# Fusing the base projection and the experts' first layer into one stage, with the experts' second layer as plain products and weight splits in a ring of halves

## The chip, the cores and the metric

The kernel runs on one core of a Trainium2 chip. The metric is the device time of one execution in microseconds (us). A core has a matrix engine (TensorE, PE in the profile, with its weight loads as PEld), a vector engine (VectorE, DVE), a scalar engine (ScalarE, ACT), a general one (GpSimd, POOL) and a queue engine (SyncE, SP). Each runs its own instructions in order, and they meet through semaphores. On-chip memory has 128 partitions; the matrix engine writes its sums into 8 banks of 512 fp32 values per partition.

## The reference, cut to what matters

```python
# x: (32, 64, 1024) fp32; cond: 32 indices in 0..15
a = einsum('bct,bcd->bdt', x, L0_cond_weights[cond])            # mixing, 64x64 per sample
h = silu(a @ w1.T + b1) * (a @ w2.T + b2)                        # "up": 1024 -> 2 x 1024
x = x + h @ w3.T + b3                                            # "down"
y = x @ W + (x @ lora_A[cond]) @ lora_B[cond]                    # "lin", rank 16 per sample
base = y @ W_org.T
coeffs = softmax((y.mean(1) @ Wq.T) @ lora_keys.T / sqrt(128))   # 8 experts per sample
hh = einsum('bsi,eir->bser', y, lora_down)                       # "expin": 1024 -> 8 x 64
x = x + base + einsum('be,bser,ero->bso', coeffs, hh, lora_up)   # "expup": 512 -> 1024
```

## The kernel before

The 2048 tokens go in two halves of 1024 (`HALVES`), each in two tiles of 512 (`TN`). Activations lie transposed: features on partitions, tokens along the row. A half runs through seven stages (`KINDS`, line 46): `up0`, `up1`, `down`, `lin`, `expin`, `base`, `expup`. Before `up0` comes the mixing (`mixing`, 128 small products of 128x128 fp32 per half).

Each stage is a 2 by 2 block product done with Strassen-Winograd: 7 products (`PRODUCTS`) instead of 8, of the four weight blocks W11, W12, W21, W22 and the four activation blocks, and of their sums. The sums S1 to S4 of activations (`s_sum`) and T1 to T4 of weights (`t_sums`) are made on DVE. Every operand is split into a high and a low fp32r part: ACT casts the high part (`act.copy` in `s_split` and `t_split`, lines 579 and 591), DVE subtracts it to get the low one (line 675). A product is then `groups * pairs * 3` matmuls of 128x128 weights on 512 columns (lines 450 to 452): 4 groups, 4 pairs and so 48 matmuls in a full stage, 24 in `expin` (2 groups) and in `expup` (2 pairs). A group fills one bank. ACT copies a product's banks out (`snap`) or DVE adds them to a block (`add`, line 754; with a bias, `addb`, line 766); in the up stages ACT applies silu (line 611) and DVE the gate (line 782).

The order of the work is written out by hand: each engine has a loop over the products `n`, and in it stands what that engine does beside product `n`: the splits of product `n + 1`, the rest of product `n - 1`, the sums. Splits have two buffers, used in turn by product. The weights have five buffers of 1 MB (the fifth, `WE`, holds T2). In `lin`, the rank-16 terms are two further kinds of matmul in plain fp32: `lora_in` (line 493, 8 of 128x512 per token tile) and `lora_out` (line 482, one of 128x512 for each of 16 groups). The hardware runs each fp32 matmul as two instructions. In `expin` the router (`route`) is put between products. SP issues all loads, ACT issues the stores of the result (line 639).

The parts that matter for the steps below are: the loops at the end of `scalar_engine` and `vector_engine` (what stands before what), `wait_bank_free` in `tensor_engine`, `lora_in` and `lora_out`, and the blocks `S1` and `S2`, without which product 2 of a stage can't be split.

Of the kernel before, what the change touches and what calls it, by code (L numbers as in the profile page):

```python
# [38 lines left out]
PRODUCTS = 7  # L39
# [3 lines left out]
W11, W12, W21, W22, WE = range(5)  # L43
W_OF = (W11, W21, WE, W11, W22, W12, W21)
# [4 lines left out]
NPAIR = {"expup": 2}  # L49
NGROUP = {"expin": 2}  # L50
LAST = NSTAGE * PRODUCTS - 1


def np_of(s):
    return NPAIR.get(STAGES[s][1], 4)


def ng_of(s):
    return NGROUP.get(STAGES[s][1], 4)

# [5 lines left out]
def phase_of(h, kind, i):  # L66
    return stage_of(h, kind) * PRODUCTS + i


def groups_of(s, j):  # L70
    n = ng_of(s) // 2
    return range(j * n, (j + 1) * n)
# [3 lines left out]
def act_first(n):  # L76
    s, i = divmod(n, PRODUCTS)
    kind = STAGES[s][1]
    if kind in ("up0", "up1"):
        if i in (0, 2, 3):  # L80
            return [("snap", n, 0)] if i != 2 else [("snap", n, 0)] + [("silu", n - 1, g) for g in groups_of(s, 1)]
    if kind in ("lin", "expin") and i in (0, 2, 3, 4):
        return [("snap", n, 0)]
    return []


def act_second(n):
    s, i = divmod(n, PRODUCTS)
    kind = STAGES[s][1]
    if kind in ("up0", "up1"):  # L90
        if i in (0, 2, 3):
            return [("snap", n, 1)]
        if i == 1:
            return [("silu", n, g) for g in groups_of(s, 0)]
        if i == 6:
            return [("silu", n, g) for g in range(ng_of(s))]
    if kind in ("lin", "expin") and i in (0, 2, 3, 4):
        return [("snap", n, 1)]
    return []


def dve_part(n, j):
    s, i = divmod(n, PRODUCTS)
    kind = STAGES[s][1]
    if kind in ("up0", "up1"):
        if i in (1, 5, 6):
            return [("add", n, j)]
        return [("gate", n, g) for g in groups_of(s, j)] if i == 4 else []
    if kind == "down":
        return [("add", n, j)] if i in (0, 2, 3) else [("addb", n, g) for g in groups_of(s, j)]  # L110
    if kind in ("lin", "expin"):
        return [("add", n, j)] if i in (1, 5, 6) else []
    return [("add", n, j)]


def dve_post(n):
    s, i = divmod(n, PRODUCTS)
    kind = STAGES[s][1]
    if kind in ("up0", "up1") and i == 6:
        return [("gate", n, g) for g in range(ng_of(s))]  # L120
    if kind == "expin":
        return {4: [("scale", n, 0)], 5: [("scale", n, 1)], 6: [("scale", n, 3), ("scale", n, 2)]}.get(i, [])
    return []
# [3 lines left out]
GROUP_AT, SNAP_AT, SUM_AT = {}, {}, {}  # L127
for _n in range(LAST + 1):
    for _g in range(ng_of(_n // PRODUCTS)):
        GROUP_AT[_n, _g] = len(GROUP_AT) + 1  # L130
    for _what in act_first(_n) + act_second(_n):
        SNAP_AT[_what] = len(SNAP_AT) + 1
    for _what in dve_part(_n, 0) + dve_part(_n, 1) + dve_post(_n):
        SUM_AT[_what] = len(SUM_AT) + 1


def group_end(n):
    return GROUP_AT[n, ng_of(n // PRODUCTS) - 1]


def t_at(n, j):
    return 2 * n + j + 1


S_ORDER = {"S1": 1, "S2": 2, "S4": 3, "S3": 4}


def s_at(s, name):
    return 4 * s + S_ORDER[name]


T_ORDER = ("T1", "T2", "T3", "T4")


def tmade_at(s, name, j):
    k = T_ORDER.index(name)
    return 8 * s + (2 * j + k + 1 if k < 2 else 5 + 2 * (k - 2) + j)


def build(nc, x_pairs, x_t, idx, cond_t, b_upgate, b_down, lora_a, lora_b, keys_t, wq_t,  # L160
          w_up0, w_up1, w_down, w_lin, w_expin, w_base, w_expup, out_t):
    w_dram = {"up0": w_up0, "up1": w_up1, "down": w_down, "lin": w_lin, "expin": w_expin,
              "base": w_base, "expup": w_expup}
# [769 lines left out]
```

## Time and profile before

| | |
|---|---|
| median of 3 runs | 1109.57 us (1109.15 to 1111.01) |
| profiled execution | 1113.7 us |
| its span, first to last instruction | 1112.0 us |
| PE busy | 1036.3 us (93%) |
| DVE busy | 832.0 us (75%) |
| ACT busy | 433.4 us (39%) |
| mean granted clock of PE | 0.977 of 2.4 GHz |

Matmuls are pipelined: a record of 0.39 us overlaps the next, which begins 0.23 us later, so the busy time of a matmul line counts more than it occupies. What a stage costs is read from its length, and what is lost in it from the matmuls that come late. "issue" as releaser is a wait for which the profile shows no engine.

### The profile page before, as it was taken

The page shows a single profiled execution, that of the slowest core. Times are in us where ns is not written, and L with a number is a line of the kernel's source. Part 1 is how long each engine was busy: PE and PEld are TensorE (multiplying, and loading weights), DVE is VectorE, ACT ScalarE, POOL GpSimd, SP SyncE. Part 2 cuts the span into 40 slices and gives each one's busy share as a digit, 9 for nine tenths or more (in the row PEclk, how much of TensorE's full clock was granted, in tenths as well). Part 3 has the DMA queues.
Part 4 walks back from the last instruction along what each step waited for, and adds up shares of the span by engine and source line. Part 5 has one row for each costly group of instructions (what it writes and reads, how often), then busy time and mean ns, then how long its engine had stood idle before and what let it go on. Part 6 is the DMA issues. An engine that isn't in the chain of part 4 may idle for free. (4 is left out here: it accounts for less than half of the span.)

```text
span 1112.0 us, 12040 instructions
## 1 busy us (share of the span) xinstructions
PE 1036.3 (93%) x4468; PEld 831.6 (75%) x4468; DVE 832.0 (75%) x681; ACT 433.4 (39%) x419; POOL 30.4 (3%) x39
## 2 busy tenths in 40 slices
PE   6999999889999979899889999997999998998988
PEld 6778788676687767688688887885866876776876
DVE  2886877976664789967848679689765747899686
ACT  5363454323233263423245445434322533532331
POOL 1400000110000000000000000002000000000000
PEclk9999999999999989899999999999999999999999
DMA  8122062131011031010750211601300110301113
GB/s 281 61 83 89 1 227 76 45 126 38 1 38 38 1 101 51 19 38 20 273 181 9 105 57 40 247 19 55 116 36 1 38 38 0 133 19 38 39 38 114
DMA packets 25032, 81.50 MB, mean 73 GB/s; under 512 B 2690, under 2 KB 6802, under 8 KB 19858
## 3 DMA queue, kind: packets, MB, share of 16 engines
q1 hardware_dynamic: 20370, 71.84, 18.5%
q10 hardware_dynamic: 4512, 8.91, 2.3%
q8 instruction: 36, 0.59, 0.2%
q14 instruction: 18, 0.15, 0.0%
q0 software_dynamic: 96, 0.02, 0.0%
HBM read 72.37 MB, written 8.39 MB: 73 GB/s over the span
## 5 line engine op out<-in xcount | busy, mean ns | idle before, releaser
L450 PE MATMUL banks<-s_hi,t_hi 128*128 128x512 f32 x1344 | 548.7, 408 | 54.2 <-DVE r L754 27.6
L451 PE MATMUL banks<-s_lo,t_hi 128*128 128x512 f32 x1344 | 531.3, 395 | 0.0
L452 PE MATMUL banks<-s_hi,t_lo 128*128 128x512 f32 x1344 | 530.8, 395 | 0.0
L450 PEld LDWEIGHTS banks<-s_hi,t_hi 128*128 128x128 f32 x1344 | 257.3, 191 | 123.0 <-issue 57.9
L451 PEld LDWEIGHTS banks<-s_lo,t_hi 128*128 128x128 f32 x1344 | 257.4, 192 | 61.4 <-issue 8.6
L452 PEld LDWEIGHTS banks<-s_hi,t_lo 128*128 128x128 f32 x1344 | 256.8, 191 | 55.0
L675 DVE TENSOR_TENSOR t_lo<-w,t_hi 128x1024 fp32r<-128x1024 f32 (+1 forms) x196 | 200.8, 1065 | 3.2 <-ACT t_hi L591 3.2
L754 DVE TENSOR_TENSOR r<-banks,r 128x1024 f32<-128x1024 f32 (+1 forms) x116 | 132.3, 1163 | 93.1 <-PE banks L452 59.9
L579 ACT CAST s_hi<-st 128x2048 fp32r<-128x2048 f32 (+1 forms) x56 | 99.9, 1785 | 232.7 <-PE banks L452 111.3
L591 ACT CAST t_hi<-w 128x1024 fp32r<-128x1024 f32 (+1 forms) x196 | 171.3, 923 | 3.4 <-PE banks L452 3.3
L675 DVE TENSOR_TENSOR s_lo<-st,s_hi 128x2048 fp32r<-128x2048 f32 (+1 forms) x56 | 119.5, 2134 | 56.8 <-ACT s_hi L579 56.8
L579 ACT CAST s_hi<-r 128x2048 fp32r<-128x2048 f32 (+1 forms) x42 | 75.0, 1787 | 201.5 <-PE banks L452 158.6
L675 DVE TENSOR_TENSOR s_lo<-r,s_hi 128x2048 fp32r<-128x2048 f32 (+1 forms) x42 | 89.8, 2138 | 78.1 <-ACT s_hi L579 78.1
L605 ACT COPY r<-banks 128x1024 f32<-128x1024 f32 (+1 forms) x56 | 49.9, 891 | 130.4 <-PE banks L452 113.0
L510 PE MATMUL banks<-mix,st 128*128 128x128 f32 x256 | 33.5, 296 | 14.1 <-POOL mix L321 9.2
L510 PEld LDWEIGHTS banks<-mix,st 128*128 128x128 f32 x256 | 32.7, 211 | 14.8 <-issue 14.7
L611 ACT ACTIVATE r<-r,b_up_sb 128x512 f32<-128x512 f32 x32 | 21.0, 714 | 48.1 <-DVE r L754 48.1
L435 POOL TENSOR_TENSOR r<-r 128x512 f32<-128x512 f32 x2 | 14.2, 7082 | 713.6 <-DMA r<-lora_b_in 713.6
L482 PE MATMUL banks<-xr,r 128*128 128x512 f32 x64 | 32.6, 590 | 0.0
L708 DVE TENSOR_TENSOR w<-w 128x1024 f32<-128x1024 f32 (+1 forms) x28 | 30.1, 1074 | 2.9 <-issue 0.4
L733 DVE TENSOR_TENSOR st<-st,r 128x2048 f32<-128x2048 f32 (+1 forms) x14 | 30.0, 2142 | 1.5
L493 PE MATMUL banks<-r 128*128 128x512 f32 x64 | 28.3, 594 | 2.7 <-issue 2.7
(53 smaller groups left out, 340.9 us busy)
## 6 DMA issues: line engine op xcount, KB each, us to landing
w<-w_up_in SPq DMA_DIRECT2D x16, 1024.0 KB, 4.9
st<-x_pairs_in SPq DMA_DIRECT2D x16, 512.0 KB, 6.2
w<-w_down_in SPq DMA_DIRECT2D x8, 1024.0 KB, 5.1
r<-x_t_in SPq DMA_DIRECT2D x8, 1024.0 KB, 7.2
w<-w_lin_in SPq DMA_DIRECT2D x8, 1024.0 KB, 4.7
w<-w_base_in SPq DMA_DIRECT2D x8, 1024.0 KB, 4.7
out_t<-r ACTq DMA_DIRECT2D x16, 512.0 KB, 3.5
w<-w_expin_in SPq DMA_DIRECT2D x8, 512.0 KB, 3.2
```

The source lines that it names most:

```text
L450: pe.matmul(out, w_hi, x_hi, start=start, stop=False, skip_group_check=True)
L451: pe.matmul(out, w_hi, x_lo, start=False, stop=False, skip_group_check=True)
L452: return pe.matmul(out, w_lo, x_hi, start=False, stop=stop, skip_group_check=True)
L482: return pe.matmul(banks[:, bank_of(n, g), :], lora_b_sb[:, t, col:col + P], xr[:, t, :], start=start, stop=stop, skip_group_check=True)
L510: last = pe.matmul(out[:, k, :], x_c[:, k * P:(k + 1) * P], mix[:, c, :], start=True, stop=True)
L579: act.copy(s_hi[:, n % 2, s_range(n)], s_source(n)).then_inc(s_hi_done, 1)
L591: act.copy(t_hi[:, n % 2, cols], w[:, W_OF[i], cols]).then_inc(t_hi_done, 1)
L605: act.copy(half_block(n, at), half_banks(n, at)).then_inc(snapped, 1)
L675: return dve.tensor_tensor(out, value, hi.bitcast(F32), ALU.subtract)
L708: dve.tensor_tensor(w[:, WE, cols], w[:, W22, cols], w[:, W11, cols], ALU.subtract).then_inc(t_made, 1)
L733: dve.tensor_tensor(upper, lower, a[0], ALU.subtract).then_inc(s_made, 1)
L754: dve.tensor_tensor(half_block(n, at), half_banks(n, at), half_block(n, at), ALU.add).then_inc(summed, 1)
```

## The change

- Stages: `expin` and `base` become one stage, `exp`. Both multiply the same activations, so the seven splits and four sums of them are made once. A product has 6 groups: 4 of base, 2 of the experts' first layer (72 matmuls). The experts' four output blocks stay in `r[:, 8:10]`, gathered with ACT copies (`esnap`) and adds (`eadd`). Their weights lie in buffers of their own, `we`.
- `expup`: the Strassen form goes; 4 plain products of 48 matmuls, on two activation splits and two weight blocks. The number of products falls from 98 to 80.
- Weight splits lie in a ring of 4 halves (`T_ID`); a half is split again as soon as the groups that read it are done, not the whole product.
- Beside a product: S1 and S2 now stand ahead of the weight sums, T3 and T4 move from products 1 and 2 to products 3 and 4, S4 moves behind the splits of product 3, and on ACT the split of the next activations stands ahead of snaps and silus.
- `lora_in`: each 128x512 matmul becomes four of 128 rows x 32 weight columns on 128 tokens, since each sample needs only its own 16 rank columns. `lora_out`: one of 128x512 becomes two of 64 rows on 256 tokens, in two turns per pair of groups, with a semaphore (`lora_crossed`) between the turns.
- Loads: both `gather_a` now run at the start of `down`; `gather_b` waits until both are laid out; `x` of the second half is loaded during `exp`. The router's weights take the place of `cond_sb` once the mixing blocks are made.
- The 16 stores of 512 KB go from ACT's queue to POOL's; SP waits for them at the end.

```diff
-KINDS = ("up0", "up1", "down", "lin", "expin", "base", "expup")
+KINDS = ("up0", "up1", "down", "lin", "exp", "expup")
+PRODUCTS = [(s, i) for s in range(NSTAGE) for i in range(4 if STAGES[s][1] == "expup" else 7)]
...
+def groups_in(n):
+    return 6 if kind_of(n) == "exp" else 4
...
-        t_hi, t_lo = sb("t_hi", [P, 2, 16 * P], F32R), sb("t_lo", [P, 2, 16 * P], F32R)
-        w = sb("w", [P, 5, 16 * P])
+        t_hi, t_lo = sb("t_hi", [P, 4, 8 * P], F32R), sb("t_lo", [P, 4, 8 * P], F32R)
+        w = sb("w", [P, 4, 16 * P])
+        we = sb("we", [P, 4, 8 * P])
...
-            def lora_out(n, g, start, stop):
-                i = n % PRODUCTS
-                t, col = (1 if i >= 5 else 0), (g if i in (1, 6) else 4 + g) * P
-                return pe.matmul(banks[:, bank_of(n, g), :], lora_b_sb[:, t, col:col + P], xr[:, t, :],
-                                 start=start, stop=stop, skip_group_check=True)
+            def lora_out(n, pair):
+                s, i = PRODUCTS[n]
+                t = 1 if i >= 5 else 0
+                for turn in range(2):
+                    if turn == 1:
+                        pe.wait_ge(lora_crossed, 2 * (4 * STAGES[s][0] + (1, 4, 5, 6).index(i)) + pair + 1)
+                    for j in range(2):
+                        g, rows = 2 * pair + (turn + j) % 2, slice(64 * j, 64 * (j + 1))
+                        col = (g if i in (1, 6) else 4 + g) * P
+                        last = pe.matmul(banks[:, bank_of(n, g), j * 2 * P:(j + 1) * 2 * P],
+                                         lora_b_sb[rows, t, col:col + P], xr[rows, t, :],
+                                         start=False, stop=False, skip_group_check=True)
+                    if turn == 0:
+                        last.then_inc(lora_crossed, 1)
+                return last
...
-                    last = pe.matmul(banks[:, bank, :], lora_a_sb[:, t, k, :], x1, start=(k == 0), stop=(k == K - 1))
+                    for q in range(4):
+                        cols = slice(32 * q, 32 * (q + 1))
+                        last = pe.matmul(banks[cols, bank, 0:P], lora_a_sb[:, t, k, cols], x1[:, q * P:(q + 1) * P],
+                                         start=(k == 0), stop=(k == K - 1), skip_group_check=True)
...
             for n in range(LAST + 1):                      # scalar_engine
-                if n > 0:
-                    take(act_second(n - 1))
-                if n < LAST:
-                    if (n + 1) % (len(KINDS) * PRODUCTS):
-                        s_split(n + 1)
-                    t_split(n + 1)
+                if n < LAST and kind_of(n + 1) != "up0" or i < 6 and kind == "up0":
+                    s_split(n + 1)
+                if n > 0:
+                    take(act_snaps(n - 1))
+                if n < LAST:
+                    t_split(n + 1, 0)
+                if n > 0:
+                    take(act_silus(n - 1))
...
-                act.dma_start(dst, src).then_inc(stored[b], 16)
+                pool.dma_start(dst, src).then_inc(stored[b], 16)
```

On ACT, this is what stands around the start of `down` in the first half, before. The names: `s_hi` and `t_hi` are the high parts of activations and weights, ACTIVATE is the silu of `up1`'s last product.

```order
L579 CAST s_hi<-r 128x2048
L591 CAST t_hi<-w 128x1024 x2
L611 ACTIVATE r<-r,b_up_sb 128x512 x4
L579 CAST s_hi<-r 128x2048
L591 CAST t_hi<-w 128x1024 x2
L579 CAST s_hi<-st 128x2048
```

And in the changed kernel:

```order
L803 CAST s_hi<-r 128x2048
L822 CAST t_hi<-w 128x1024 x2
L803 CAST s_hi<-r 128x2048
L822 CAST t_hi<-w 128x1024 x2
L842 ACTIVATE r<-r,b_up_sb 128x512 x4
L803 CAST s_hi<-st 128x2048
```

The splits for product 1 of `down` now stand ahead of the four silus.

On DVE, products 1 to 3 of `down` in the first half, before. L711 is T3, L716 is T4, L737 is S4, L740 is S3, L766 and L754 take the banks.

```order
L675 TENSOR_TENSOR s_lo<-st,s_hi 128x2048
L675 TENSOR_TENSOR t_lo<-w,t_hi 128x1024 x2
L711 TENSOR_TENSOR w<-w 128x1024 x2
L766 SCALAR_TENSOR_TENSOR r<-banks,b_dn_sb,r 128x512 x4
L737 TENSOR_TENSOR st<-r,st 128x2048
L675 TENSOR_TENSOR s_lo<-st,s_hi 128x2048
L675 TENSOR_TENSOR t_lo<-w,t_hi 128x1024 x2
L716 TENSOR_TENSOR w<-w 128x1024 x2
L754 TENSOR_TENSOR r<-banks,r 128x1024 x2
L740 TENSOR_TENSOR st<-r 128x2048
```

In the changed kernel (L973 is every weight sum, L929 is S4, L932 is S3, L999 and L989 take the banks):

```order
L891 TENSOR_TENSOR s_lo<-st,s_hi 128x2048
L891 TENSOR_TENSOR t_lo<-we,t_hi 128x1024 x2
L999 SCALAR_TENSOR_TENSOR r<-banks,b_dn_sb,r 128x512 x4
L891 TENSOR_TENSOR s_lo<-st,s_hi 128x2048
L891 TENSOR_TENSOR t_lo<-w,t_hi 128x1024 x2
L929 TENSOR_TENSOR st<-r,st 128x2048
L989 TENSOR_TENSOR r<-banks,r 128x1024 x2
L891 TENSOR_TENSOR s_lo<-st,s_hi 128x2048
L891 TENSOR_TENSOR t_lo<-w,t_hi 128x1024 x2
L932 TENSOR_TENSOR st<-r 128x2048
L973 TENSOR_TENSOR w<-w 128x1024 x2
```

Between the splits of product 2 and the add of product 2's banks (L754, now L989), the four instructions of T3 and T4 are gone; T3 stands behind the splits of product 4.

## Rows read from the trace of the kernel before

**Rows 1.** Windows, by stage: stretch, length, PE, PEld, DVE, ACT, POOL busy, PEclk, DMA.

```profile
27.30:106.50 79.20, 76.84 (x339) 63.02 (x338) 61.59 (x45) 36.96 (x33) 11.71 (x16) 1.00 0.23 84
106.50:185.10 78.60, 76.73 (x337) 62.91 (x336) 62.20 (x48) 38.08 (x36) 0.00 (x0) 1.00 0.30 107
185.10:278.40 93.30, 84.82 (x353) 66.74 (x352) 73.39 (x62) 33.83 (x29) 6.97 (x1) 0.98 0.19 63
278.40:376.00 97.60, 97.60 (x387) 72.21 (x385) 60.44 (x43) 29.68 (x26) 0.00 (x0) 1.00 0.07 22
376.00:428.00 52.00, 44.99 (x196) 36.03 (x195) 44.82 (x43) 27.17 (x32) 0.00 (x0) 0.93 0.24 81
428.00:514.50 86.50, 81.30 (x338) 66.23 (x338) 69.64 (x55) 24.82 (x21) 0.00 (x0) 0.94 0.08 25
514.50:578.00 63.50, 56.48 (x298) 48.60 (x296) 47.78 (x48) 23.14 (x28) 0.00 (x0) 0.95 0.56 199
578.00:654.30 76.30, 76.30 (x340) 63.17 (x339) 56.33 (x41) 37.11 (x33) 0.00 (x0) 1.00 0.18 63
654.30:734.50 80.20, 78.05 (x338) 64.14 (x337) 62.60 (x48) 38.19 (x36) 0.00 (x0) 0.98 0.29 105
...
1062.30:1112.00 49.70, 41.29 (x169) 33.32 (x167) 38.69 (x41) 12.54 (x18) 0.00 (x0) 0.93 0.23 85
```

**Rows 2.** Timeline of PE: start, length, instruction; in brackets the wait before it.

```profile
130.25 0.47 PE L450 MATMUL banks<-s_hi,t_hi 128*128 128x512 f32 x1 [1.81 <-issue]
...
225.34 0.77 PE L450 MATMUL banks<-s_hi,t_hi 128*128 128x512 f32 x1 [5.02 <-DVE r L754]
...
393.80 0.76 PE L450 MATMUL banks<-s_hi,t_hi 128*128 128x512 f32 x1 [4.66 <-DVE s_lo L675]
```

**Rows 3.** Timeline of ACT, start of up1.

```profile
108.48 2.56 ACT L611 ACTIVATE r<-r,b_up_sb 128x512 f32<-128x512 f32 x4 [8.83 <-DVE r L754]
110.95 1.89 ACT L579 CAST s_hi<-r 128x2048 fp32r<-128x2048 f32 x1
```

**Rows 4.** Timeline of DVE, down, product 2.

```profile
210.13 2.35 DVE L711 TENSOR_TENSOR w<-w 128x1024 f32<-128x1024 f32 x2
212.40 2.72 DVE L766 SCALAR_TENSOR_TENSOR r<-banks,b_dn_sb,r 128x512 f32<-128x512 f32 x4
215.03 2.28 DVE L737 TENSOR_TENSOR st<-r,st 128x2048 f32<-128x2048 f32 x1
...
221.71 2.35 DVE L716 TENSOR_TENSOR w<-w 128x1024 f32<-128x1024 f32 x2
```

**Rows 5.** Timeline of PE: after a wait, lora_in twice, lora_out, router, last matmul.

```profile
226.76 0.63 PE L450 MATMUL banks<-s_hi,t_hi 128*128 128x512 f32 x1
...
271.88 3.67 PE L493 MATMUL banks<-r 128*128 128x512 f32 x8 [1.33 <-issue]
...
289.74 7.03 PE L493 MATMUL banks<-r 128*128 128x512 f32 x16
...
299.34 1.02 PE L482 MATMUL banks<-xr,r 128*128 128x512 f32 x2
...
387.29 1.85 PE L520 MATMUL banks<-y_sum,wq_sb 128*128 128x16 f32 x16
...
1106.97 0.39 PE L452 MATMUL banks<-s_hi,t_lo 128*128 128x512 f32 x1
```

**Rows 6.** Timeline of PE: mixing of the first half, first of the second.

```profile
9.23 14.68 PE L510 MATMUL banks<-mix,st 128*128 128x128 f32 x112 [9.23 <-POOL mix L321]
...
558.20 3.73 PE L510 MATMUL banks<-mix,st 128*128 128x128 f32 x32
```

**Rows 7.** Issues of DMAs, KB each, median us from issue to landing.

```profile
out_t<-r ACTq DMA_DIRECT2D x16, 512.0 KB, 3.5
...
b_up_sb<-b_upgate_in POOLq DMA_DIRECT2D x1, 8.0 KB, 3.5
```

**Rows 8.** Timeline of SP's queue: 15 of the 16 issues of gather_b.

```profile
200.56 15.82 SPq L373 DMA_DIRECT2D r<-lora_b_in  x15
```

More of the change, by code:

```diff
@@ L87, in act_second @@
[L87 to L97, printed above, removed]
-        return [("snap", n, 1)]
[L99 to L105, printed above, removed]
+    return FIRST[stage_of(h, kind)] + i
@@ new lines, in groups_of @@
+def groups_of(j):
+    return range(2 * j, 2 * j + 2)
+S_ID, S_LAST = {}, []
+T_ID, T_LAST = {}, []
+for _n, (_s, _i) in enumerate(PRODUCTS):
+    _up = kind_of(_n) == "expup"
+    if _up and _i >= 2:
+        S_ID[_n] = S_ID[_n - (1 if _i == 2 else 3)]
+    else:
+        S_ID[_n] = len(S_LAST)
+        S_LAST.append(_n)
+    S_LAST[S_ID[_n]] = _n
+    for _j in range(groups_in(_n) // 2):
+        if _up and _i % 2 == 1:
+            T_ID[_n, _j] = T_ID[_n - 1, _j]
+        else:
+            T_ID[_n, _j] = len(T_LAST)
+            T_LAST.append(None)
+        T_LAST[T_ID[_n, _j]] = (_n, 2 * _j + 1)
@@ L109, in dve_part @@
     if kind == "down":
-        return [("add", n, j)] if i in (0, 2, 3) else [("addb", n, g) for g in groups_of(s, j)]
-    if kind in ("lin", "expin"):
+        return [("add", n, j)] if i in (0, 2, 3) else [("addb", n, g) for g in groups_of(j)]
+    if kind == "lin":
         return [("add", n, j)] if i in (1, 5, 6) else []
     return [("add", n, j)]
-def dve_post(n):
[L117 to L123, printed above, removed]
@@ L127, with dve_after @@
-GROUP_AT, SNAP_AT, SUM_AT = {}, {}, {}
+def dve_after(n):
+    i, kind = PRODUCTS[n][1], kind_of(n)
+    if kind == "exp":
+        return [("eadd", n, k) for k in range(len(E_ADDS[i]))] + ([("scale", n, 2)] if i == 6 else [])
+    return [] if kind == "expup" and i == 3 else dve_half(n, 1)
+def dve_post(n):
+    i, kind = PRODUCTS[n][1], kind_of(n)
+    if kind in UPS and i == 6:
+        return [("gate", n, g) for g in range(4)]
+    return [("scale", n, 3)] if kind == "exp" and i == 5 else []
@@ L161, in build @@
           w_up0, w_up1, w_down, w_lin, w_expin, w_base, w_expup, out_t):
-    w_dram = {"up0": w_up0, "up1": w_up1, "down": w_down, "lin": w_lin, "expin": w_expin,
-              "base": w_base, "expup": w_expup}
+    w_dram = {"up0": w_up0, "up1": w_up1, "down": w_down, "lin": w_lin, "exp": w_base, "expup": w_expup}
+    row_of = {"11": 0, "12": 1, "21": 2, "22": 3, "21 again": 2, "lower": 0, "upper": 1}
     with ExitStack() as ctx:
@@ L532, in route @@
                         rows = coef_rows[:, 2 * k:2 * k + 2, :].rearrange("b e r -> b (e r)")
[L533 removed]
+                        last = pe.matmul(coef_bank[:, k * BH:(k + 1) * BH], rows, ident[:, :],
                                          start=True, stop=True)
```

854 lines of the change are left out of this document (517 added, 337 removed).

## Prediction

> **What bounds the kernel now.** I read the windows view first, cut at the first matmul of each stage, then the late matmuls in PE's timeline, then what DVE and ACT did just before each. The windows show PE busy in nearly every stage while DVE is at 62 to 86%: second half's `up0` is 76.3 us with PE busy for all of it [rows 1]. It holds 7 x 48 = 336 product matmuls, so one costs 76.3 / 336 = 0.2271 us, and the kernel's 4032 cost 915.6. That is 82% of the span; PE bounds it, and the rest (1112.0 - 915.6 = 196.4) is what the change can touch. By stage, as length less 0.2271 for each of its matmuls [rows 1]: start 27.3; `up0` 2.9 and 0.0; `up1` 2.3 and 3.9; `down` with the first `lora_in` 17.0 twice; `lin` 21.3 twice; `expin` (168 matmuls, 38.15) 13.9; `base` 10.2; `expup` with the mixing 25.3; last stretch 11.6. The second half's `down` to `base` (734.5 to 1062.3) is 327.8 us, the first's 329.4.
>
> These extras are of four kinds. (1) Waits for splits and sums: product 2 late by 1.81 in `up1`, product 3 by 5.02 in `down`, product 2 by 4.66 in `expin` [rows 2]. (2) After the longer of them PE runs at the lower of its two clock levels for a while: a matmul 1.4 us after the wait of 5.02 has a record of 0.63, where the kernel's last has 0.39 [rows 2, 5]; at 1.2 GHz 512 columns take 0.43 instead of 0.2271, and the stretches with long waits show a mean clock of 0.93 to 0.98 [rows 1]. (3) Plain fp32 matmuls for rank 16: `lora_in` takes 7.03 per tile; a `lora_in` instruction 7.03 / 16 = 0.44; a `lora_out` pair ends 1.02 after it began, and with 0.44 between the two starts a record lasts 0.58 [rows 5]. (4) Mixing: 112 instructions in 14.68, so 0.131 each and 16.8 for a half's 128 [rows 6].
>
> **Product matmuls.** `exp` has 7 x 72 = 504 where `expin` and `base` had 168 + 336: the same. `expup` has 4 x 48 = 192 where it had 168: 24 more per half, 48 x 0.2271 = +10.9 us. All 4080 cost 926.6.
>
> **Waits in up0, up1 and down.** On ACT, four silus (2.56 us) end at 111.04, and only then does the split for product 1 begin (the cast of 1.89 at 110.95) [rows 3]; now it stands ahead, so DVE's low parts, the gates, S1 and S2 all come about 3 us sooner, more than the 1.81 by which product 2 was late. In `up0` the cast of S2 now runs beside the weight sums. In `down` product 3 waited for the add of product 2's banks, which stood behind T3 (2.35), the bias adds, S4, two splits and T4 (2.35) [rows 4]. Without T3 and T4 (4.7 together) nearly all of the 5.02 goes. What is late next: T3 now stands behind the splits of product 4. From the start of product 3, the cast for product 4 takes 1.9 [rows 3], its s_lo 2.2 and S3 2.2 (both as S4), its two t_lo 2.3 and T3 2.3 (both as T4) [rows 4], and the add that frees its first bank 1.2, half of such a pair: 12.1, where product 3 lasts 48 x 0.2271 = 10.9. I put 1.4 per half, with 0 to 5.02 as ends. With shorter waits the slow clock goes too. So `up0` 0.2 and 0, `up1` 0.1 twice, `down` 1.4 of waits.
>
> **lora_in.** PE still waits for the bank of `down`'s last product, 1.33 [rows 5]. Then each tile has 64 instructions of 32 columns on 128 tokens instead of 16 on 512. No row shows parts of the array at work side by side. One after the other they cost 64 x 0.131 = 8.4 (the mixing's rate, same 128 columns); four strips at once 2.1. A worse end: each costs the 0.44 of today's, 28. The nearest row, by tokens and by passes, is the mixing's, and the disjoint strips speak for overlap, since today's records already overlap (0.39 long, 0.2271 apart); between 2.1 and 8.4 I take 3 per tile, so 12 for four.
>
> The Trainium skill, "TensorE: Matmul & The Clock Gate", section on packing small matmuls, gives 3.07 times for four row tiles and 2.38 for three column tiles; by 3.07 the estimate would be 7.03 / 3.07 = 2.3 per tile. No run here shows it. Against it, "TensorEngine Tiling (Array Packing)", key properties, says that a change of tiling mode drains the engine, and this change switches some 40 times.
>
> **lora_out.** A product has 8 instructions at 0.44 = 3.5 us today. Now 16 of half the length: 16 x 0.22 = 3.5 one after the other, 1.8 two at once. To that two waits for `lora_crossed` per product. Their bound is the part of a record that outlasts its cadence, 0.58 - 0.44 = 0.14 [rows 5], up to twice that with the semaphore: 0.3 to 0.6. So 2.1 to 4.1; I take 2.4, times 8 = 19.2 (today 28).
>
> **exp and expup.** The wait of 4.66 and its like come from too little PE time (5.4 us a product) to cover S1, S2 and the splits. A product of `exp` is 16.3 us of PE. The heaviest, product 0, has on DVE: by the durations of rows 4, three bank adds (3.5), s_lo (2.2), three t_lo (3.4), the y sum (2.2), S1 and S2 (4.5), three weight sums (3.4): 19.2 us, over by 3, but product 1 has 9 to 10 and S2 is needed only at product 2, 32.6 us after the start. The next ones come to 15, 12, 14, 12 and 11. ACT has 5 per product. So no wait, but the router's matmuls, 1.85 for the first 16 [rows 5] and about as much for the other ten with their pauses: 3.5 per half. `expup`'s second activation split needs the last scale: bank add, scale, cast, s_lo is 6.5 us beneath a product of 10.9. Its weights load during `exp`. S sums (6 of 2048 columns per half) and 8.5 activation splits per half vanish, some 30 us of DVE per half; they lie beneath PE and are worth only the waits named.
>
> **Mixing of the second half.** Today it lasts from 558.20 to 578.0 [rows 1, 6], 19.8, of which 16.8 is matmuls. x comes earlier and two banks free earlier; I take 17.3.
>
> **Loads.** A gather issues one DMA per 15.82 / 15 = 1.05 us [rows 8]. Both `gather_a` (17 us) precede `gather_b` (17 us), which now starts when T3 of `down` is made, about 44 us into the stage (three products and 10.9), and ends at 61; `lin` needs it beyond 76. W12 of `lin` is queued behind it on SP and lands some 5 us after its issue, at about 66, and T1, which wants it, stands behind the splits made at the start of product 6, so at 65 + 6 = 71. Hidden, with 5 us to spare; if it overshoots, T1, T2 and the add that frees the bank for `lora_in` are late by that much.
>
> **Tail.** The last matmul begins at 1106.97 [rows 5]; 5.0 follow: one add and a store of 3.5 [rows 7]. The store now comes from POOL, whose 8 KB DMA took 3.5 to land where one of 512 KB took 3.5 from ACT. Between +0 and +3.5; I take +2, so 7. The Trainium skill, "DMA: Bandwidth & Descriptors", fits 2.0 us plus bytes / 436e3 for this path, an estimate of 3.2 and so no loss.
>
> **Sum.** First half: 27.3 + 76.5 + 76.4 + (76.3 + 1.4 + 1.3) + 76.3 + (114.5 + 3.5) + 43.6 + 17.3 = 514.4. Second: 76.3 + 76.4 + 79.0 + 76.3 + 118.0 + 43.6 + 7.0 = 476.6. With `lora_in` 12 and `lora_out` 19.2: 1022.2. A walk misses small waits, so I add 4: span 1026, against 1112.0. The profiled execution was 1.7 above its span (1113.7) and 4.1 above the median, so the median should be 1026 + 1.7 - 4.1 = 1024, which is 7.7% faster.
>
> **Rivals.**
> - Tiles don't overlap: `lora_in` 8.4 and `lora_out` 4.1. The sum without both is 991; 991 + 33.6 + 32.8 + 4 = 1061 span, 1059. For it: nothing in the trace shows overlap. Against: disjoint strips, separate banks and the care taken by `lora_crossed` not to write one place twice.
> - The waits stay, only moved: the order doesn't do what it says. Then `up0` and `up1` keep their 9.1 and `down` its 17.0 - 7.0 = 10.0 twice (my sum has 5.8 for all of these), and `exp`'s heavy product 0 adds its 3 twice. Span 1026 + 23 + 6 = 1055, 1053. For it: DVE has 3 us too much in product 0, and all adds stand in one queue. Against: slack of 5 us at each deadline that I walked.
> - The clock drops to the lower level around the tiled matmuls, as after waits [rows 5]: 20 blocks, each followed by as much loss as one long wait brings, some 1.5 (7 matmuls at 0.43), +30: 1054. For it: the slow stretch after the wait of 5.02. Against: `lin` runs at 1.00 with 97.6 of 97.6 busy [rows 1].
> - Slower than before: a tiled instruction costs the whole of today's 0.44. 256 of `lora_in` then take 113, 128 of `lora_out` 56 plus 4: 991 + 173 + 4 = 1168. It decides from (1112 - 995) / 384 = 0.30 us per instruction. For it: small matmuls do have a floor (16 of 16 columns take 1.85, 0.12 each [rows 5]). Against: that floor is a third of 0.30.
>
> **How the numbers follow.** Forecast 60%, no overlap 15%, waits stay 12%, clock 8%, slower 3%, no change 2%. Low end: `lora_in` 2.1, `lora_out` 2.1, tail 5, no missed waits: 991 - 2 + 8.4 + 16.8 = 1014, less 2.4 is 1012; I go to 1008 for waits in `down` at 0. High end 1060, which takes in the first three rivals. Within 1008 to 1060 lie eight in ten. What a measurement here can tell from no change is 0.2%: faster 0.96, same 0.01, slower 0.03.
>
> **What would show it.** In the profile after: `up0` to `down` at 76 to 79 us net of `lora_in`; `exp` at 118 with no wait of PE over 1 us; `expup` at 43.6; 16 tiled instructions of `lora_out` in 2.4 or 4; a `lora_in` tile in 3 or 8; 17 us of mixing. The forecast is wrong if `lora_in` stays at 7 or if PE waits for DVE inside `exp`.

## The result, and the profile after

The changed kernel takes 1020.13 us, the median of four runs (1020.12 to 1022.75), beside 1110.09 for the kernel before on the same chip: 0.9196 times, 95% interval 0.9179 to 0.9213. The forecast was 1024 with a range of 1008 to 1060. The profiled execution took 1020.12 with a span of 1018.4, where the forecast's sum had 1026 and before it was 1112.0.

First the busy times of the changed kernel's engines, as shares of its span.

```profile
PE 996.7 (98%) x4772; PEld 816.0 (80%) x4772; DVE 743.1 (73%) x574; ACT 391.2 (38%) x349; POOL 33.8 (3%) x55
```

PE is busy for 98% of a span that is 94 us shorter. Next its windows by stage, the first half's six (`up0`, `up1`, `down` with the first `lora_in`, `lin`, `exp`, `expup` with the mixing), then the second half's `expup` with the tail; columns as in [rows 1].

```profile
24.46:100.70 76.24, 76.24 (x339) 63.17 (x338) 61.59 (x45) 37.28 (x34) 15.11 (x16) 1.00 0.24 87
100.70:176.90 76.20, 76.20 (x338) 63.09 (x337) 62.33 (x48) 37.28 (x35) 0.00 (x0) 1.00 0.30 111
176.90:258.10 81.20, 78.44 (x402) 64.53 (x400) 73.18 (x62) 34.22 (x30) 1.29 (x1) 1.00 0.27 91
258.10:349.40 91.30, 90.76 (x469) 68.89 (x465) 61.97 (x42) 32.22 (x28) 0.00 (x0) 1.00 0.17 58
349.40:467.20 117.80, 117.80 (x533) 97.41 (x532) 90.33 (x72) 37.20 (x32) 0.00 (x0) 1.00 0.21 76
467.20:526.40 59.20, 58.19 (x322) 50.39 (x320) 25.91 (x20) 14.80 (x13) 5.82 (x8) 1.00 0.34 125
...
969.10:1018.40 49.30, 43.72 (x193) 35.87 (x192) 16.71 (x13) 3.81 (x3) 5.81 (x8) 0.96 0.23 86
```

Beside [rows 1]: `up0` went from 79.2 to 76.24, `up1` from 78.6 to 76.20, `down` from 93.3 to 81.2, `lin` from 97.6 to 91.3, and `expin` with `base` (52.0 + 86.5 = 138.5) to 117.8. PE is busy for the whole of `up0`, `up1` and `exp`. The granted clock was 0.93 to 0.98 in six of the ten windows of [rows 1]; now it is 1.00 in each stage (the last window holds the idle time behind the last matmul). A window's counts take in records that reach over its ends, so stages are compared by length.

The timeline of PE has the terms of the forecast one by one (columns as in [rows 2]): the one DVE wait left, `lora_in` with its wait and the second tile, a block of `lora_out`, the router, the mixing's 7.30, and the last matmul.

```profile
221.99 0.47 PE L634 MATMUL banks<-s_hi,t_hi 128*128 128x512 f32 x1 [1.42 <-DVE r L989]
...
256.21 1.95 PE L710 MATMUL banks<-r 128*32 128x128 f32 x64 [1.34 <-issue]
...
269.20 1.95 PE L710 MATMUL banks<-r 128*32 128x128 f32 x64
...
276.75 1.47 PE L693 MATMUL banks<-xr,r 64*128 64x256 f32 x8
...
414.79 1.85 PE L740 MATMUL banks<-y_sum,cond_sb 128*128 128x16 f32 x16
...
510.70 7.30 PE L728 MATMUL banks<-mix,st 128*128 128x128 f32 x64
...
1012.43 0.39 PE L636 MATMUL banks<-s_hi,t_lo 128*128 128x512 f32 x1
```

No wait of PE for DVE is over 1 us but one in each half's `down`, of 1.42 and 1.39: the 5.02 and the 4.66 of [rows 2] and the 1.81 are gone. A tile of `lora_in` took 7.03 [rows 5] and takes 1.95. The chain of waits into 221.99 names what is late in `down` (start, length, what):

```profile
209.73 1.92 ACT s_hi L803
211.65 0.02 issue
211.68 1.93 DVE s_lo L891
213.61 0.28 issue
213.88 1.32 DVE t_lo L891 x2
215.20 0.95 issue
216.16 2.29 DVE st L932
218.44 2.27 DVE w L973 x2
220.71 1.15 DVE r L989
221.86 0.14 issue
221.99 0.47 PE banks L634
```

That is the forecast's sum for `down` step by step: cast, `s_lo`, two `t_lo`, S3, T3, and the add that frees the bank, behind which product 4 stands.

Where the 93.6 us of span went, by stage, both halves together. An excess is the time from a stage's first product matmul to the next stage's, less 0.2267 for each product matmul in it (differences are taken before rounding):

```
                                          before   after   difference
up0 and up1, waits and slow clock            9.6     0.2       -9.4
down, waits and slow clock                  18.3     3.4      -14.9
lora_in, with the wait before it            29.9    11.0      -18.9
lora_out                                    29.8    26.3       -3.6
expin and base; now exp                     46.0     6.9      -39.2
expup: waits; now 48 more matmuls           12.5    10.9       -1.6
mixing of the second half                                      -4.1
start                                       27.3    24.5       -2.9
from the last matmul to the end              5.0     6.0       +1.0
sum                                                           -93.6
```

Four tenths lies in the merged stage. It issues the 504 product matmuls that `expin` and `base` had between them, with the router's 3.5 us per half as all that is left over. Not all of the 39.2 is the merge: in b1 below, the new order alone takes 6.5 from the two old stages. The other 32.7 came with the merge, and no run has the merge without the ring of weight halves and the new loads, or these without it.

### The profile page after: what moved, and what is told of

Same layout as the page of the kernel before. It is cut to its first block, busy times and chain, and to the rows that moved or that the text cites. A ratio compares the mean times of both kernels' runs of the same rounds, so it can differ in the third digit from the quotient of the medians.

```text
span 1018.4 us, 12337 instructions
## 1 busy us (share of the span) xinstructions
PE 996.7 (98%) x4772; PEld 816.0 (80%) x4772; DVE 743.1 (73%) x574; ACT 391.2 (38%) x349; POOL 33.8 (3%) x55
## 4 chain that ended last, share of the span: by engine, by line
PE 95%; DVE 2%; DMA 1%; issue 1%; ACT 0%; POOL 0%; POOLq 0%; ACTq 0%
PE banks L634 30%; PE banks L635 29%; PE banks L636 29%; PE banks L728 2%; PE banks L693 2%; PE banks L710 1%; DMA cond_sb<-cond_t_in 1%; DMA st<-x_pairs_in 1%; DVE st L932 0%; DVE w L973 0%; DVE s_lo L891 0%; ACT s_hi L803 0%; DVE r L989 0%; PE banks L740 0%; DVE t_lo L891 0%
## 5 line engine op out<-in xcount | busy, mean ns | idle before, releaser
L989 DVE TENSOR_TENSOR r<-banks,r 128x1024 f32<-128x1024 f32 x92 | 111.3, 1220 | 106.3 <-PE banks L636 79.9
L891 DVE TENSOR_TENSOR t_lo<-w,t_hi 128x1024 fp32r<-128x1024 f32 x132 | 156.5, 1218 | 3.2 <-ACT t_hi L822 3.2
L803 ACT CAST s_hi<-st 128x2048 fp32r<-128x2048 f32 x40 | 76.5, 1912 | 199.0 <-PE banks L636 132.8
L822 ACT CAST t_hi<-w 128x1024 fp32r<-128x1024 f32 x132 | 133.3, 1049 | 50.9 <-PE banks L636 50.8
L803 ACT CAST s_hi<-r 128x2048 fp32r<-128x2048 f32 x34 | 65.0, 1912 | 212.5 <-PE banks L636 144.5
L891 DVE TENSOR_TENSOR s_lo<-st,s_hi 128x2048 fp32r<-128x2048 f32 x40 | 91.6, 2291 | 51.9 <-ACT s_hi L803 51.7
L891 DVE TENSOR_TENSOR s_lo<-r,s_hi 128x2048 fp32r<-128x2048 f32 x34 | 77.8, 2290 | 57.7 <-ACT s_hi L803 57.7
L973 DVE TENSOR_TENSOR w<-w 128x1024 f32<-128x1024 f32 x48 | 57.2, 1219 | 0.0
L834 ACT COPY r<-banks 128x1024 f32<-128x1024 f32 x40 | 40.4, 1009 | 24.9 <-PE banks L636 20.6
L1009 DVE TENSOR_TENSOR r<-banks,r 128x1024 f32<-128x1024 f32 x14 | 17.0, 1223 | 28.8 <-PE banks L636 28.8
L891 DVE TENSOR_TENSOR t_lo<-we,t_hi 128x1024 fp32r<-128x1024 f32 x30 | 35.9, 1219 | 0.0
L617 POOL DMA_DIRECT2D out_t<-r x16 | 11.6, 727 | 530.1 <-DVE r L989 530.1
L999 DVE SCALAR_TENSOR_TENSOR r<-banks,b_dn_sb,r 128x512 f32<-128x512 f32 x32 | 22.3, 744 | 7.6 <-PE banks L636 7.6
```

The source lines that it names most:

```text
L803: act.copy(s_hi[:, S_ID[n] % 2, :], s_source(n)).then_inc(s_hi_done, 1)
L822: act.copy(t_hi[:, T_ID[n, j] % 4, :], t_source(n, j)).then_inc(t_hi_done, 1)
L834: act.copy(half_block(n, at), half_banks(n, at)).then_inc(snapped, 1)
L891: return dve.tensor_tensor(out, value, hi.bitcast(F32), ALU.subtract)
L973: dve.tensor_tensor(out, left, right, ALU.subtract).then_inc(t_made, 1)
L989: dve.tensor_tensor(half_block(n, at), half_banks(n, at), half_block(n, at), ALU.add).then_inc(summed, 1)
```

## The experiments

A difference in us to the changed kernel is the difference of the ratios times the 1110 of the kernel before. The changed kernel's own interval is 0.9179 to 0.9213, 1.9 us to either side, so a difference under some 2.6 us says nothing by itself.

**e1: the four strips one after another.** The loop over strips goes outside the loop over k.

```diff
-                for k in range(K):
-                    x1 = act_blocks(s)[2 * t + k // 4][:, k % 4 * TN:(k % 4 + 1) * TN]
-                    for q in range(4):
+                for q in range(4):
+                    for k in range(K):
+                        x1 = act_blocks(s)[2 * t + k // 4][:, k % 4 * TN:(k % 4 + 1) * TN]
```

> The changed kernel with lora_in's loops turned: strip by strip, eight k in each, so that neighbouring instructions work on the same 32 columns of the array. Theory (the four strips run at once only because neighbours lie on different columns): a tile goes from 2.05 us to 64 x 0.107 to 0.131 = 6.8 to 8.4, four tiles, so +19 to +25 us. Rival (an instruction with a quarter of the tokens and columns is simply four times cheaper): no change, within 1 us.

1036.54 us, 0.9328 (0.9311 to 0.9345): +14.7. A tile in its timeline, with the same wait ahead:

```profile
255.87 5.93 PE L710 MATMUL banks<-r 128*32 128x128 f32 x64 [1.34 <-issue]
```

5.93 for the same 64 instructions that take 1.95 when neighbours write different strips: 0.093 each instead of 0.030 by these records, 0.090 and 0.027 by the mean steps between starts. The mean of e1 is itself too low for a pure series: within a strip its instructions start 0.109 apart, and only at the three places where one strip follows another do they come closer, down to 0.005. So 0.109 against 0.027, 4.1 times, is the gain of the strips, and all four work side by side. My price for the series was too high (8.4, from the mixing's 0.131). That 0.131 held the slow clock: of the 112 instructions of [rows 6], 19 fill the first 4.06 us, 0.21 each, and in the changed kernel the mixing's instruction takes 7.30 / 64 = 0.114.

**e2: `lora_out` on the whole array.** `xr` is masked on 128 rows again, and a group gets one pair of 128x512 instructions.

```diff
-                for turn in range(2):
-                    if turn == 1:
-                        pe.wait_ge(lora_crossed, ...)
-                    for j in range(2):
-                        g, rows = 2 * pair + (turn + j) % 2, slice(64 * j, 64 * (j + 1))
-                        last = pe.matmul(banks[..., j * 2 * P:(j + 1) * 2 * P], lora_b_sb[rows, ...], xr[rows, t, :], ...)
+                for g in (2 * pair, 2 * pair + 1):
+                    last = pe.matmul(banks[:, bank_of(n, g), :], lora_b_sb[:, t, col:col + P], xr_of[t], ...)
```

> The changed kernel with lora_out as before: one 128x512 matmul per group, no crossing wait, no row tiles. Theory (the row tiles run two at once, and most of that gain goes to the wait between turns and to changes of tile shape): a product loses 3.63 instead of 3.25, so +3 us in all. Rival (the row tiles are worth their full half, 1.75 us per product, and something else eats it): +10 us or more.

1022.64 us, 0.9193 (0.9175 to 0.9211): -0.3, no difference, where I had expected +3. Its block in the timeline:

```profile
278.86 1.88 PE L690 MATMUL banks<-xr,r 128*128 128x512 f32 x4
```

A whole product's excess is 3.53 where the changed kernel's is 3.25, so 2.2 us in all eight; but its first product matmul starts at 26.63 and the changed kernel's at 24.46, a scatter of the start as large as the effect. The times leave it undecided; the traces put the row tiles' whole gain at 2.2 us. The four instructions start 0.43 apart, so 1.72 of a block's 3.53 / 2 = 1.77 is their own: a block that does not change the array's shape has almost no fixed part.

**e3: the two turns apart.** The first turn is issued ahead of the pair's last three product matmuls, the second behind them, so that nobody waits at the crossing.

```diff
                     for p in range(4):
                         last = product(n, g, p, fresh and p == 0, p == 3)
-                    if lora and g % 2 == 1:
+                        if lora and g % 2 == 1 and p == 2:
...
-                        lora_out(n, g // 2).then_inc(group_done, 2)
+                            lora_out(n, g // 2, 0)
+                    if lora and g % 2 == 1:
+                        lora_out(n, g // 2, 1).then_inc(group_done, 2)
```

> The changed kernel with the first turn of lora_out put ahead of the last three product matmuls of the pair, so that the wait for lora_crossed is over when the second turn comes. Theory (the crossing wait costs 0.47 us, 16 times, and a change between whole-array and row-tile matmuls costs under 0.1): -7 us. Rival (each change of shape costs 0.15 to 0.35, and there are 32 more of them): from -2 to +4 us.

1021.85 us, 0.9194 (0.9178 to 0.9210): -0.2, no difference: the rival's range, not the theory's -7. Two blocks of four instead of one of eight:

```profile
275.87 0.70 PE L693 MATMUL banks<-xr,r 64*128 64x256 f32 x4
...
277.39 0.70 PE L693 MATMUL banks<-xr,r 64*128 64x256 f32 x4
```

Per product 3.41 instead of 3.25. The wait is gone: both turns' first loads now wait 0.35 for "issue", as the first turn's did before. It is paid back by entering and leaving the tiled shape twice as often. With e10 below the terms of a block can be estimated. A turn's four instructions cost 0.43 (e10). A turn alone costs 3.41 / 4 = 0.85, so going into the tiled shape and out of it makes some 0.42. A block of both turns costs 1.64 (13.15 per half for 8 blocks), which leaves 1.64 - 0.86 - 0.42 = 0.36 for the wait at the crossing. The estimate takes an instruction to cost 0.108 in a block of four too; e10's own blocks, which have no wait at the crossing, give 0.46 for the way in and out.

The crossing has a row of its own in the changed kernel's timeline of PE's weight loads: the second turn's first load waits 0.47 for the first turn's results.

```profile
277.52 0.30 PEld L693 LDWEIGHTS banks<-xr,r 64*128 64x128 f32 x4 [0.47 <-PE banks L693]
```

**e4: ACT in the old order.** Only the place of snaps and silus against the splits goes back.

```diff
+                if n > 0:
+                    take(act_snaps(n - 1))
+                if n > 0:
+                    take(act_silus(n - 1))
                 if n < LAST and kind_of(n + 1) != "up0" or i < 6 and kind == "up0":
                     s_split(n + 1)
-                if n > 0:
-                    take(act_snaps(n - 1))
                 if n < LAST:
                     t_split(n + 1, 0)
-                if n > 0:
-                    take(act_silus(n - 1))
```

> The changed kernel with ACT's old order: snaps and silus of the last product ahead of the next activations' split. Theory (this order is what cured the late product 2 in up1 and down): product 2 is late again by 1.8 to 2.3 us in four stages, and the clock may fall after it, so +8 to +12 us. Rival (moving the weight sums on DVE alone cured it): 0 to +2 us.

1031.74 us, 0.9282 (0.9266 to 0.9299): +9.5. The timeline of PE has the old wait in `up1` back, and one in `down`:

```profile
124.85 0.47 PE L634 MATMUL banks<-s_hi,t_hi 128*128 128x512 f32 x1 [1.81 <-issue]
...
205.03 0.47 PE L634 MATMUL banks<-s_hi,t_hi 128*128 128x512 f32 x1 [2.12 <-issue]
```

The 1.81 is that of [rows 2] to the digit. The late products of `up1` cost 1.98 + 1.74 us in the first half, the 1.74 in slow matmuls behind the wait, and 1.98 in the second, where none follow. `down` is 2.4 and 2.7 longer than in the changed kernel, the second half's with a wait of 2.48. So the order on ACT removed the late product 2, and not the ring of weight halves.

**e5: the weight sums where they were.** T3 and T4 go back beside products 1 and 2.

```diff
-found += {3: [(s, "T3", 0), (s, "T3", 1)], 4: [(s, "T4", 0), (s, "T4", 1)]}.get(i, [])
+found += {1: [(s, "T3", 0), (s, "T3", 1)], 2: [(s, "T4", 0), (s, "T4", 1)]}.get(i, [])
```

> The changed kernel with T3 and T4 back beside products 1 and 2 in up0, up1, down and lin. Theory (the 5.02 us of product 3 in down came from these 4.7 us standing ahead of the bank's add): product 3 of down is late by some 2 to 4 us in both halves, product 4 less late than the 1.42 now, so +3 to +8 us. Rival (the other moves on DVE, S4 behind the splits, cured it): 0, or a gain of 2 where T3 no longer delays product 4.

1030.39 us, 0.9272 (0.9257 to 0.9288): +8.4. Product 3 of `down` is late again, in either half, and after it come slow matmuls:

```profile
214.76 0.47 PE L634 MATMUL banks<-s_hi,t_hi 128*128 128x512 f32 x1 [3.97 <-DVE r L989]
...
215.81 0.63 PE L634 MATMUL banks<-s_hi,t_hi 128*128 128x512 f32 x1
...
721.22 0.77 PE L634 MATMUL banks<-s_hi,t_hi 128*128 128x512 f32 x1 [4.31 <-DVE r L989]
```

And its timeline of DVE shows why, a T sum of two halves ahead of the bank add:

```profile
208.93 2.29 DVE L929 TENSOR_TENSOR st<-r,st 128x2048 f32<-128x2048 f32 x1
211.13 2.35 DVE L973 TENSOR_TENSOR w<-w,we 128x1024 f32<-128x1024 f32 x2
213.40 2.35 DVE L989 TENSOR_TENSOR r<-banks,r 128x1024 f32<-128x1024 f32 x2
```

Products 2 and 3 of `down` are 4.13 + 1.71 and 4.47 + 2.92 us over their matmuls in the two halves, 13.2 in all, where the changed kernel has 3.4 in `down`. The waits are 8.3 of that, and most of the rest is the slow clock behind them: seven matmuls behind the first wait have records of 0.63, as the row above from 215.81, and behind the second there are more.

**e6: in `down`, a product's own adds ahead of the T sums.**

```diff
+                if kind == "down":
+                    take(dve_own(n)[0])
                 if kind != "exp":
                     for what in t_sums_beside(n):
                         t_sum(*what)
-                take(dve_own(n)[0])
+                if kind != "down":
+                    take(dve_own(n)[0])
```

> The changed kernel with down's bank adds ahead of the weight sums beside each product. Theory (product 4's late start of 1.42 and the 1.34 before lora_in both wait for an add that stands behind weight sums on DVE): both vanish in both halves, -5.5 us. Rival (the sums, now later, delay lin's splits, or the wait before lora_in has another cause): -3 to 0 us.

1015.14 us, 0.9138 (0.9122 to 0.9153): -6.4. Its timeline of PE has no wait ahead of the tile of `lora_in`, nor in front of product 4:

```profile
254.36 1.95 PE L710 MATMUL banks<-r 128*32 128x128 f32 x64
```

The add that frees product 4's bank now goes ahead of T3, as its timeline of DVE shows:

```profile
217.37 2.29 DVE L932 TENSOR_TENSOR st<-r 128x2048 f32<-128x2048 f32 x1
219.57 1.22 DVE L989 TENSOR_TENSOR r<-banks,r 128x1024 f32<-128x1024 f32 x1
220.71 2.35 DVE L973 TENSOR_TENSOR w<-w 128x1024 f32<-128x1024 f32 x2
```

Nothing else came late. The two waits of each half, 1.42 and 1.34, make 5.5; from start to start of the products, `down` is 6.2 us shorter in both halves together, and the remaining 0.2 lies within the noise.

**e8: the router's weights read at the start again**, as extra traffic into a buffer that nothing reads yet.

```diff
             for block in ("21", "12", "22"):
                 load_w(0, block)
+            sp.dma_start(we[:, 0, :], wq_t).then_inc(early_wq, 16)
```

> The changed kernel with the 512 KB of router weights loaded once more at the start, behind the first weights, as before the change (into a buffer not yet in use). Theory (the 2.8 us that the start has gained come from this transfer no longer sharing the DMA engines with the last x chunks): the first product matmul comes at about 27 instead of 24.5. Rival (the start scatters by itself): no shift beyond what other runs of the changed kernel show, and the mixing stays in one piece.

1020.68 us, 0.9184 (0.9169 to 0.9200): -1.3, within the two intervals. Its profiled start is later (first product matmul at 26.83), its median is not. In the ten traces of kernels without the load the first product matmul came between 24.06 and 26.63, and in three with it at 26.83, 26.98 and 27.3. The traces also show the path: the last piece of x, which the last 16 mixing instructions need, lands between 21.6 and 24.6 without the load and at 24.8, 24.95 and 25.3 with it, and wherever PE waits there it goes on 0.24 to 0.25 after that landing. So the missing load probably brings the start forward, but by an amount that the scatter covers, and the times don't confirm it.

**b1: the kernel before, with the new order alone** (no merged stage, no tiled matmuls, no ring).

```diff
-                if n > 0:
-                    take(act_second(n - 1))
                 if n < LAST:
...
                         s_split(n + 1)
+                if n > 0:
+                    take([a for a in act_second(n - 1) if a[0] == "snap"])
                 if n < LAST:
                     t_split(n + 1)
+                if n > 0:
+                    take([a for a in act_second(n - 1) if a[0] == "silu"])
...
-                if i in (2, 3):
-                    s_sum(s, "S4" if i == 2 else "S3")
...
-                if i in (1, 2) or n == 0:
-                    t_sums(s, i)
-                if i == 6 and s + 1 < NSTAGE:
-                    t_sums(s + 1, 0)
+                if i in (2, 3):
+                    s_sum(s, "S4" if i == 2 else "S3")
+                if i in (3, 4) or n == 0:
+                    t_sums(s, i - 2 if i else 0)
+                if i == 6 and s + 1 < NSTAGE:
+                    t_sums(s + 1, 0)
```

> The kernel before with the new order alone: on ACT the next activations' split ahead of snaps and silus, on DVE S1 and S2 ahead of the weight sums, S4 behind the splits, T3 and T4 beside products 3 and 4, in all seven stages. Theory (the waits in up0, up1 and down are a matter of order, those of expin too little PE time): up0, up1 and down lose 9.1 + 2 x 10.0 less 5.8 = 23 us, base some of its 10, expin and expup keep most of theirs: -25 to -35 us against before. Rival (the order helps only together with the ring of halves): under -10.

1072.62 us, 0.9649 (0.9631 to 0.9668): -39.0 to the kernel before, more than I expected. The order is 39 of the 90 us by itself. By its trace, 37.7 us shorter, `up0` and `up1` lose 9.4, `down` 14.9, `expin` and `base` 6.5 and `expup` 6.2. What it can't remove are waits of the short stages; its timeline of PE in `expin` and `expup`:

```profile
380.68 0.76 PE L450 MATMUL banks<-s_hi,t_hi 128*128 128x512 f32 x1 [4.66 <-DVE s_lo L678]
399.56 0.47 PE L450 MATMUL banks<-s_hi,t_hi 128*128 128x512 f32 x1 [1.55 <-ACT r L605]
...
515.71 0.47 PE L450 MATMUL banks<-s_hi,t_hi 128*128 128x512 f32 x1 [1.37 <-DVE r L757]
```

The 4.66 is that of [rows 2], unmoved by the order, and gone only in the kernel with the merged stage. `base`, which had 10.2 over its matmuls, fell to 6.2 by order alone.

**e10: `lora_out` in one block per product.** Both pairs' first turns, then both pairs' second turns; product 5's block stands ahead of its groups, where it follows product 4's with no product matmul between.

```diff
-            def lora_out(n, pair):
+            def lora_out(n):
...
+                if i == 5:
+                    for g in range(4):
+                        wait_bank_free(n, g)
                 for turn in range(2):
-                    if turn == 1:
-                        pe.wait_ge(lora_crossed, ...)
-                    for j in range(2):
+                    for pair in range(2):
+                        if turn == 1:
+                            pe.wait_ge(lora_crossed, ...)
+                        for j in range(2):
...
+                if lora and i == 5:
+                    lora_out(n)
                 for g in range(groups_in(n)):
```

> The changed kernel with lora_out in one block per product (turn one for both pairs, then turn two): behind the last group for products 1, 4 and 6, ahead of the first for product 5, so that 4's and 5's adjoin. Theory (of the 3.25 us per product, a change of tile shape in and out costs 0.42 and a crossing wait 0.34, each twice; the work itself is 0.43 per turn): 1 and 6 fall to about 2.1, 4 and 5 together from 6.4 to 3.9, so -9 us in all. Rival (the later group ends make DVE's adds and ACT's snaps late, and PE waits for them): -4 to +4 us.

1011.58 us, 0.9110 (0.9091 to 0.9128): -9.5, as expected. Its blocks:

```profile
282.50 2.00 PE L701 MATMUL banks<-xr,r 64*128 64x256 f32 x16
...
317.33 3.72 PE L701 MATMUL banks<-xr,r 64*128 64x256 f32 x32
```

Sixteen more instructions cost 3.72 - 2.00 = 1.72, so 0.108 each, against 0.22, half of today's 0.44, if they ran one after another. In the trace they start in pairs, 0.007 apart within a pair and 0.215 from pair to pair: the two row tiles work side by side. At that rate a block of eight (1.47) would be 0.86: the remainder is what grouping saves. `lora_out` fell from 13.15 to 8.44 per half, 2.1 per product, the forecast's lower bound.

**e7: the second half's stores issued by SP.** One run of 1019.9 us, so this rests on the trace. The loop that is added stands at the end of SP's program.

```diff
-                for u in range(4):
-                    store(h, u, 0)
-                    store(h, u, 1)
+                if h + 1 < HALVES:
+                    for u in range(4):
+                        store(h, u, 0)
+                        store(h, u, 1)
...
+            for u in range(4):
+                store(1, u, 0)
+                store(1, u, 1)
```

> The changed kernel with the second half's stores issued by SP instead of POOL. Theory (5.95 us pass from the start of the last matmul to the end, where it was 5.0 with stores from ACT, because POOL issues and lands later): 5.0 again, 0.9 us less. Rival (it is the add or the transfer itself): 5.9.

The last matmul in e7, and then the last add and the last store's issue in the changed kernel:

```profile
1013.11 0.39 PE L652 MATMUL banks<-s_hi,t_lo 128*128 128x512 f32 x1
```

```profile
1012.86 1.23 DVE L989 TENSOR_TENSOR r<-banks,r 128x1024 f32<-128x1024 f32 x1 [4.22 <-PE banks L636]
...
1014.73 0.72 POOL L617 DMA_DIRECT2D out_t<-r  x1 [5.04 <-DVE r L989]
```

e7's span ends 5.07 after that matmul begins, the changed kernel's 5.97 after. The store's record on POOL begins 0.64 after the add's end (1014.09) and lasts 0.72. In e7 the add ends at 1014.77 and SP's record begins at 1014.79, so 0.62 of the 0.9 lies ahead of the issue. The landings differ little: in the median 3.2 from issue for POOL's stores and 2.8 for SP's in e7, 3.5 for ACT's [rows 7].

**e11: e6, e7 and e10 together.**

> The three together: down's bank adds ahead of its weight sums, one block of lora_out per product, the second half's stores from SP. If they add up: -6 - 9 - 1 = -16 us against the changed kernel, so about 1004 where before takes 1110. If the later group ends of lora_out cost waits, -8 to -12.

1004.28 us (1004.03 to 1005.89), 0.9048 (0.9029 to 0.9067): -16.4, the sum of its parts (6.4 + 0.9 + 9.5 = 16.8) within the intervals. It beats both kernels, with a mean granted clock of 1.000 over its span of 1002.4.

## Why the forecast was right, step by step

1. **The bound: right.** A product matmul takes 0.2267 in every undisturbed stage, as 76.3 / 336 had it, and the four stages of PE time alone came out at 76.2 to 76.3 where I had 76.3 to 76.5.
2. **The waits of `up1` and `down`: right, with their causes.** e4 and e5 bring back the one and the other (+9.5, +8.4). What is late next was named with its size: 1.4 taken, 1.42 measured (1.58 from start to start). The exact hit is partly luck, since the steps I listed make 12.1 against 10.9, so 1.2, and I put 1.4. The 1.34 ahead of `lora_in` stayed; e6 shows that the order of adds and T sums on DVE held both, and that both could have gone.
3. **`lora_in`: right in mechanism, mis-sized.** Taken 3 per tile, measured 2.05 and 2.10, which was my bound for four strips at once. That is -3.7 in four. The 3 was a choice between the bounds 2.1 and 8.4 with nothing measured behind it. By e1 four strips work at 0.109 / 0.027 = 4.1 times the rate of one by the steps between starts, and at 5.93 / 1.95 = 3.0 times by the two records. The Trainium skill, "TensorE: Matmul & The Clock Gate", section "Measured speedup vs the span model", gives 3.07 for four row tiles and 2.38 for three column tiles. It doesn't list four column strips; by the steps they do better here than its 3.07, and the records' 3.0 comes from an order that is not a pure series.
4. **`lora_out`: the term that was too small.** Taken 2.4 per product, measured 13.15 / 4 = 3.3, +7.1 in eight. The two tiles do overlap (0.108 per instruction instead of 0.22), and the two crossings of a product make some 0.7, over the 0.3 to 0.6 that I gave them. What I left out is the price of going from the whole array to tiles and back, twice per product, some 0.4 each time. I had cited, beside `lora_in`, that a change of tiling mode drains the engine (the Trainium skill, "TensorEngine Tiling (Array Packing)", "Key Properties"), and had given it no term; by e3 and e10 it costs 0.42 to 0.46 per block, where e2's untiled block has 0.05. That the 0.4 is such a drain is the page's reading; the runs show the price. With it my sum would have been 4 x 0.43 + 0.7 + 0.8 = 3.2.
5. **`exp`: right, to 0.2 us.** 118.0 taken, 117.8 measured. Product 0's 19.2 us of DVE under 16.3 of PE did no harm. b1 shows that the order alone leaves the 4.66, and that I understated the order: it removed 39.0 us alone where I expected 25 to 35, since it also shortened waits in `base` (10.2 to 6.2 in the first half) and `expup` (12.5 to 6.3 in both). Which of the moves on ACT and DVE did that, no run shows.
6. **`expup` and the mixing.** `expup` had no waits, as forecast. The second half's mixing took 15.7 where I took 17.3 (-1.6): my 0.131 per instruction carried the slow clock.
7. **Start and tail.** The start came 2.8 sooner, with no term for it in the sum; the last piece of x landed sooner, and e8 leaves open how much of that is the load that moved. The tail is 5.97 where I took 7 (-1.0); e7 puts the POOL issue at +0.9.
8. **The allowance of 4 for small waits was not needed.** Product by product the trace has none.

The errors: -3.7 (`lora_in`), +7.1 (`lora_out`), -1.6 (mixing), -2.8 (start), -1.0 (tail), -4 (allowance), sum -6.0; the rest of -1.6 lies in the other stages, most of which came out 0.1 to 0.3 shorter each. 1026 - 7.6 = 1018.4. So the span missed by 7.6 with terms of both signs. The median missed by 4 only, and that is luck: I had taken off 4.1 because the profiled execution of the kernel before was that much above its median, and the changed kernel's profiled execution is at its median (1020.12 and 1020.13). With `lora_out` right and all else as it was, the median would have missed by 11.

Of the rivals, no overlap fell with e1 (it would have cost 16 in `lora_in`) and with the pairs of e10, the moved waits and the slow clock at the tiled blocks fell with the windows (1.00 in each stage, and 20 blocks per kernel without a slow matmul behind them), and the slower one with 0.03 per `lora_in` instruction against the 0.30 from which it would decide.

## What to carry to other kernels

On a kernel that its matmuls bound, ask of each late matmul which instruction stands ahead of the one it waits for, and whether anybody waits for that one: moving it behind gained 39 us here before any work was saved. Price small tiled matmuls by the block: a fixed part for changing shape and one for each hand-over between tiles, then the instructions, so one block of sixteen beats two of eight even where the tiles overlap perfectly. Merging a short stage into its neighbour paid here because the short one had too little matmul time to cover its splits and sums (5.4 us a product, with a wait of 4.66).

## What the runs showed of the hardware that was not expected

- Going into row tiles and back costs some 0.4 us per block (0.42 by e3, 0.46 by e10), and a wait for one's own results across tiles some 0.35, an estimate from e3 and e10; for small blocks these two are nearly half of the time (0.78 of 1.64).
- Four column strips of 32 take a plain fp32 instruction of 128 columns every 0.027 us, one strip every 0.109 (e1). An untiled one on 128 columns takes 0.112 by its steps (the mixing).
- Splitting `lora_out` into tiles halves its array time, and yet it gained only 2.2 us over whole-array instructions, of 8 x 3.53 = 28 (e2), and 11.6 once in blocks of sixteen (2.2 + 2 x (13.15 - 8.44)).
- A POOL subtraction of 128x512, at work beside DVE, has a record of 6.97 in [rows 1], of 1.29 in the window of `down` above and of 2.42 in b1. I have no explanation, and spans on POOL are rough.
- The clock stayed at 1.00 from the first product matmul of the changed kernel to the last, and no wait of PE between them was over 1.42 us. A wait of 1.81 had slow matmuls behind it in one half of e4 and none in the other; in e5 the 4.31 has a record of 0.77 behind it and the 3.97 one of 0.47, and slow matmuls of 0.63 follow both. Yet the waits of 2.12 and 2.48 in e4's `down` have no slow matmul behind them. So the length of a wait alone does not say what it costs.
